# Paged attention in a four-layer kernel: cached values fetched by SyncE, one transfer a page, instead of by GpSimd gathers of rows

## The reference

```python
B, S, HID = (4, 128, 512); D, HQ, HK = (128, 32, 8); PAGES, PSIZE, NPP = (64, 32, 16)
q, k, v = projections of x by Wq, Wk, Wv; q and k: RMS norm, then rotary embedding
kc = k_cache[block_table].reshape(bsz, L, HK, D)
vc = v_cache[block_table].reshape(bsz, L, HK, D)
k_all = jnp.concatenate([kc, k], axis=1)
v_all = jnp.concatenate([vc, v], axis=1)
scores = jnp.einsum('bqhd,bkhd->bhqk', q, k_all) * SCALE
scores = jnp.where(valid[:, None, None, :], scores, -1e+30)
probs = jax.nn.softmax(scores, axis=-1)
o = jnp.einsum('bhqk,bkhd->bqhd', probs, v_all)
return jnp.einsum('bse,de->bsd', o.reshape(bsz, seqlen, HQ * D), Wo)
```

## Time and profile before

| | |
|---|---|
| median of three runs | 3655.53 us |
| the profiled execution | 3660.96 us |
| its span, first to last instruction | 3659.2 us |
| mean granted TensorE clock | 0.964 |
| TensorE busy, of the span | 3193.8 us, 87% |
| VectorE, ScalarE, GpSimd busy | 1825.0, 1293.9, 1583.7 us |
| SyncE's own queue (q1), packets and bytes | 363540, 197.79 MB |
| GpSimd's queue (q0), packets and bytes | 50768, 175.71 MB |

### The profile page before, as it was taken

One profiled execution on the slowest core, in us unless ns is written; L12 is line 12 of the kernel. 1 busy time (PEld: TensorE's weight loads), 2 busy tenths in 40 slices (PEclk: granted clock), 3 DMA queues, 4 the chain that ended last, 5 costly groups with the idle time before them and its releaser, 6 DMA issues. The chain is left out here.

```text
span 3659.2 us, 66283 instructions
## 1 busy us (share of the span) xinstructions
PE 3193.8 (87%) x15248; PEld 2058.2 (56%) x15248; DVE 1825.0 (50%) x5079; ACT 1293.9 (35%) x3541; POOL 1583.7 (43%) x1336
## 2 busy tenths in 40 slices
PE   3599999999999999989999999999999976888887
PEld 2366666666666656556566666666566553444444
DVE  4254554555555555554545455445445534555555
ACT  1234443444344443433343344334433321222222
POOL 7444455555555555554555545545554410000000
PEclk8799999999999999999999999999999997999898
DMA  5533333333333333543333333333333333111110
GB/s 192 201 96 109 105 104 106 107 109 105 104 107 116 109 110 112 175 149 105 105 104 104 104 104 106 113 109 113 111 111 106 98 125 97 29 34 49 31 29 12
DMA packets 415398, 376.22 MB, mean 103 GB/s; under 512 B 83364, under 2 KB 346292, under 8 KB 414277
## 3 DMA queue, kind: packets, MB, share of 16 engines
q1 hardware_dynamic: 363540, 197.79, 18.6%
q0 software_dynamic: 50768, 175.71, 15.5%
q10 hardware_dynamic: 864, 0.63, 0.1%
HBM read 340.37 MB, written 25.17 MB: 100 GB/s over the span
## 5 line engine op out<-in xcount | busy, mean ns | idle before, releaser
L355 PEld LDWEIGHTS ps_oT<-pT,v_sb 128*128 128x128 f32 x4096 | 525.7, 195 | 427.3 <-ACT pT L425 248.4
L417 ACT ACTIVATE p_sb<-s_sb,nmax 128x544 f32<-128x544 f32 x512 | 383.2, 748 | 1017.4 <-DVE nmax L516 907.9
L355 PE MATMUL ps_oT<-pT,v_sb 128*128 128x128 f32 x4096 | 579.1, 285 | 176.7 <-ACT pT L425 145.5
L288 PE MATMUL ps_t<-wqkv,xT 128*128 128x512 f32 x1536 | 694.5, 595 | 7.6 <-DMA xT<-x1T_scratch 7.6
L182 POOL DMA_INDIRECT v_sb<-in_v_rows_w,v_row x512 | 507.2, 991 | 289.0 <-issue 127.4
L516 DVE CUSTOM_DVE_ANT_0 s_sb<-ps_s,mask,nmax_new 128x416 f32<-128x416 f32 x512 | 333.4, 651 | 353.6 <-PE ps_s L329 281.4
L312 PE MATMUL ps_t<-wo,oT 128*128 128x512 f32 x1024 | 449.9, 592 | 0.4 <-ACT oT L433 0.4
L329 PE MATMUL ps_s<-k_sb,qT 128*128 128x416 f32 x1024 | 445.9, 523 | 0.0
L288 PEld LDWEIGHTS ps_t<-wqkv,xT 128*128 128x128 f32 x1536 | 278.9, 191 | 288.4 <-issue 280.6
L197 POOL TENSOR_SCALAR ss<-ss 128x12 f32<-128x12 f32 x64 | 13.2, 206 | 965.3 <-DVE ss L494 962.8
L532 DVE TENSOR_SCALAR p_sb<-p_sb,rinv 128x544 f32<-128x544 f32 x512 | 370.0, 723 | 18.1
(11 more groups left out here) (214 smaller groups left out, 4282.5 us busy)
## 6 DMA issues: line engine op xcount, KB each, us to landing
k_sb<-in_kT SPq DMA_DIRECT2D x2048, 64.0 KB
xT<-x1T_scratch POOLq DMA_DIRECT2D x32, 256.0 KB
tab<-rope_scratch POOLq DMA_DIRECT2D x32, 256.0 KB
v_sb<-in_v_rows_w,v_row POOLq DMA_INDIRECT x512
wo<-in_wo_w POOLq DMA_DIRECT2D x2, 4096.0 KB, 15.6
v_new<-v_raw SPq DMA_DIRECT2D x128, 64.0 KB
y_scratch<-y_sb SPq DMA_DIRECT2D x32, 256.0 KB
wqkv<-in_wqkv_w SPq DMA_DIRECT2D x6, 1024.0 KB, 9.0
```

What stands on the lines that cost most here:

```text
L288: m = e.matmul(ps_t[bank_of(t)][:, :], xT[:, k, :], wqkv[:, k, 512 * t:512 * t + 512], start=k == 0, stop=k == KC - 1)
L355: e.matmul(ps_oT[:, :], v_sb[:, b % 2, c, h * D:(h + 1) * D], pT[:, u % 2, c, :], start=c == 0, stop=False)
L417: e.activation(p_sb[:, u % 2, :], s_sb[:, u % 2, :], ACT.Exp, bias=nmax[:, u % 2:u % 2 + 1], scale=-1.0, accum_out=rsum[:, u % 2:u % 2 + 1 ...
```

## The change

The cached values are no longer gathered by GpSimd. SyncE issues them, right after the keys of the same block, from the page numbers that it already holds in registers: 16 transfers of one page, 32 tokens x 512 values, into 32 of the 128 partitions of `v_sb`. Before them it waits until the block before last is weighed. The cache of values is laid out by page and half of the heads, as that of the keys was. What served the row numbers goes: `btx`, `voff`, `v_rows`, `v_row`, two GpSimd instructions and two loads in `embed`, and a copy a round. TensorE's wait for a block's values counts 16 transfers instead of 4.

```diff
@@ attention, SyncE @@
                     wait(e, scored, UNITS * r + HKH * (b - 1))
                     for j, page in enumerate(pages):
                         e.dma_start(k_sb[:, b % 2, j, :, :], A["kT"][bass.ds(page * HALVES + half, 1), :, :, :].rearrange("a d h s -> (a d) h s")).then_inc(dma_k[b % 2], 16)
+
+                    wait(e, weighed, UNITS * r + HKH * (b - 1))
+                    for j, page in enumerate(pages):
+                        at = slice(PSIZE * (j % LC), PSIZE * (j % LC) + PSIZE)
+                        e.dma_start(v_sb[at, b % 2, j // LC, :], A["v_pages"][bass.ds(page * HALVES + half, 1), :, :].rearrange("a s n -> (a s) n")).then_inc(dma_v[b % 2], 16)
@@ attention, GpSimd @@
-            def load_rows(r):
...
-            def load_v(r, b):
-
-                wait(e, weighed, UNITS * r + HKH * (b - 1))
-                e.sem_inc(passed, 1)
-                for c in range(LC):
-                    e.indirect_dma_start(out=v_sb[:, b % 2, c, :], out_offset=None, in_=A["v_rows_w"],
-                                         in_offset=bass.IndirectOffsetOnAxis(ap=v_row[:, b, c:c + 1], axis=0)).then_inc(dma_v[b % 2], 16)
-
...
                 if last(r):
-                    load_v(r, 2)
-                    load_v(r, 3)
                     return
-                rotate(r + 1, 0, lambda: load_v(r, 2))
-                load_v(r, 3)
+                rotate(r + 1, 0)
                 rotate(r + 1, 1)
-                load_rows(r + 1)
-                load_v(r + 1, 0)
 
                 e.wait_ge(raw_copied, NT * (r + 2))
                 if xg is not None:
                     load_x(xg)
                 if weights:
                     load_w(1)
-                load_v(r + 1, 1)
@@ attention, TensorE @@
                 if h == 0:
-                    e.wait_ge(dma_v[b % 2], 16 * LC * (2 * r + b // 2 + 1))
+                    e.wait_ge(dma_v[b % 2], 16 * NPP * (2 * r + b // 2 + 1))
@@ embed, GpSimd @@
-            for h in range(HALVES):
-                step(e.tensor_scalar(v_rows[:, h * B * LC:(h + 1) * B * LC], btx[:, h, :], float(PSIZE * HALVES), voff[:, h:h + 1], ALU.mult, ALU.add))
@@ laid_out @@
-    a["v_rows_w"] = i["L1_cond_v_cache"].reshape(PAGES * PSIZE * HALVES, HKH * D)
+    a["v_pages"] = i["L1_cond_v_cache"].reshape(PAGES, PSIZE, HALVES, HKH * D).transpose(0, 2, 1, 3).reshape(PAGES * HALVES, PSIZE, HKH * D)
```

More of the change, by code:

```diff
@@ L37, with attention @@
 NEG = -1e30
-def attention(nc, sb, pb, sem, wqkv, wo, dma_wqkv, dma_wo, x1T_d, tab_d, y_d, A, ident, iota, seqf, v_rows, load_beside):
+def attention(nc, sb, pb, sem, wqkv, wo, dma_wqkv, dma_wo, x1T_d, tab_d, y_d, A, ident, iota, seqf, load_beside):
     k_sb = sb("k_sb", [P, 2, NPP + 1, HKH, PSIZE], F32)
@@ L44, in attention @@
     bt = sb("bt", [1, B * NPP], I32)
-    v_row = sb("v_row", [P, GB, LC], U32)
     xT = sb("xT", [P, KC, P], F32)
@@ L82, in attention @@
     dma_vn, v_cleared = sem("dma_vn"), sem("v_cleared")
-    new_scored, new_copied, new_ready, placed, rows_ready = (sem(n) for n in ("new_scored", "new_copied", "new_ready", "placed", "rows_ready"))
+    new_scored, new_copied, new_ready, placed = (sem(n) for n in ("new_scored", "new_copied", "new_ready", "placed"))
     dma_k = [sem(f"dma_k{i}") for i in range(2)]
@@ L188, in _, with rotate @@
             parts = [[(0, 12, 0)], [(12, HQH - 12, 0), (HQH, HKH, 2)]]
-            def rotate(r, i, gathers=None):
+            def rotate(r, i):
                 h0, h1 = ((0, 12), (12, HT))[i]
@@ L213, in rotate @@
                     if half:
-                        if gathers is not None:
-                            gathers()
                         e.wait_ge(rope_step, done)
@@ L249, in _ @@
             e.wait_ge(half_made, 1)
-            load_rows(0)
-            load_v(0, 0)
-            load_v(0, 1)
             e.dma_start(wo[:, :, :], A["wo_w"][0]).then_inc(dma_wo[0], 16)
@@ L570, with embed @@
 XB = 4
-def embed(nc, sb, pb, sem, wqkv, dma_wqkv, A, x1_d, x1T_d, tab_d, ident, seqf, v_rows):
+def embed(nc, sb, pb, sem, wqkv, dma_wqkv, A, x1_d, x1T_d, tab_d, ident, seqf):
     qw = sb("qw", [P, KC, HID], I32)
@@ L600, in embed @@
     tabs = sb("tabs", [P, GROUPS, 4, D], F32)
-    btx = sb("btx", [P, HALVES, B * LC], I32)
-    voff = sb("voff", [P, HALVES], F32)
     seqi = sb("seqi", [P, HALVES * B], I32)
@@ L699, in step @@
                 e.wait_ge(chain_p, done[0])
-            e.wait_ge(dma_t, 16 * 6)
+            e.wait_ge(dma_t, 16 * 4)
             e.wait_ge(dma_c, 32)
@@ L772, in _ @@
         def _(e):
-            for to, of in ((posi, "seq_tok"), (invf, "inv_freq"), (w4, "rope_w"), (btx, "bt_rows"), (voff, "row_off"), (seqi, "seq_all")):
+            for to, of in ((posi, "seq_tok"), (invf, "inv_freq"), (w4, "rope_w"), (seqi, "seq_all")):
                 e.dma_start(to[:], A[of]).then_inc(dma_t, 16)
@@ L1368, in program @@
         seqf = sb("seqf", [P, HALVES * B], F32)
-        v_rows = sb("v_rows", [P, HALVES * B * LC], U32)
         dma_const = sem("dma_const")
@@ L1390, in program @@
                 sb, pb = tools(ctx)
-                embed(nc, sb, pb, sem, wqkv, dma_wqkv[0], A, x1_d, x1T_d, tab_d, ident, seqf, v_rows)
+                embed(nc, sb, pb, sem, wqkv, dma_wqkv[0], A, x1_d, x1T_d, tab_d, ident, seqf)
             with ExitStack() as ctx:
                 sb, pb = tools(ctx)
-                attention(nc, sb, pb, sem, wqkv, wo, dma_wqkv, dma_wo, x1T_d, tab_d, y_d, A, ident, iota, seqf, v_rows, load_beside)
+                attention(nc, sb, pb, sem, wqkv, wo, dma_wqkv, dma_wo, x1T_d, tab_d, y_d, A, ident, iota, seqf, load_beside)
             with ExitStack() as ctx:
@@ L1421, in laid_out @@
     a["inv_freq"] = rows((np.float32(1.0) / np.float32(10000.0) ** (np.arange(0, D, 2, dtype=np.float32) / np.float32(D))).astype(np.float32))
-    a["row_off"] = np.stack([(tok % PSIZE) * HALVES + h for h in range(HALVES)], 1).astype(np.float32)
     a["c_identb"] = np.eye(P, dtype=np.float32).astype(mybir.dt.np(BF))
@@ L1443, in laid_out @@
     a["block_table"] = bt.reshape(1, B * NPP)
-    a["bt_rows"] = np.repeat(np.repeat(bt.reshape(B * LC, P // PSIZE), PSIZE, axis=1).T[:, None, :], HALVES, axis=1)
     qn, kn = HQH * D, HKH * D
```

## The result

| | before | with the change |
|---|---|---|
| median | 3654.26 us (4 runs) | 4421.94 us (4 runs, 4417.09 to 4423.66) |
| span of the profiled execution | 3659.2 us | 4421.3 us |
| attention stage ends at | 3015.0 us | 3778.1 us |
| mean granted TensorE clock | 0.964 | 0.888 |

The change makes the kernel slower by a factor of 1.21 (95% interval 1.2079 to 1.2121), 768 us. The direction was forecast, and so was what sets the new time: SyncE's queue.

What follows compares the result with a forecast made beforehand. SyncE and TensorE were taken to share the bound. 1352 us of added transfers, less 37 of waits filled and 6 at the stage's end, gave +1309 us: 4965 us for the median, range 4480 to 5150 us.

Steps and rivals of the forecast that it cites:

- The bound: In the attention stage SyncE, with 1.1 us of waiting a round, is as full as TensorE; the two share the bound.
- The price of a page of values: On SyncE in the attention stage: 2048 added transfers at 0.66 us each, 1352 us.
- rival A: A page of values is issued on SyncE at the price of a page of keys, 0.44 us: 4514 us; chance 0.19.
- What else SyncE does: SyncE's existing 87.96 us a round stays, and the values' transfers bring it to 130.2 us.
- the sum: Values' transfers less waits filled and the stage's earlier end: 1352 - 37 - 6 = +1309 us.
- a possible surcharge on the values: 8% of unnamed stalls, seen in SyncE's bursts of keys, put on the values: 0.71 us a transfer, 1454 us.
- The waits filled: The values' transfers fill SyncE's present waits on TensorE in the attention stage: -36.6 us.
- The end of the stage: From SyncE's last transfer to the attention stage's end: 28.7 us instead of 34.7, 6 us less.
- The new wait: SyncE's wait, ahead of the values, for the block before last to be weighed: met on arrival, nothing taken.
- rival B: SyncE also stands at the new wait because TensorE, partly at a lower clock, weighs late: 5093 us; chance 0.11.
- TensorE's clock: In the attention stage the granted clock falls in pauses of some 42 us a round; nothing in the sum.
- Nothing for GpSimd's relief: 512 gathers of 957 ns leave GpSimd in the attention stage; taken to gain nothing.

Runs made afterwards that it cites:

- the doses above: The changed kernel with 16 page-number loads a block but no bounds check: 3899.24 us; with one load of 16 registers a block instead: 3591.18 us.

## Why the prediction was right or wrong

- **The bound** was read rightly, and the change is slower by the mechanism that was forecast. SyncE, which has no row in the table of busy times, shared the bound with TensorE, and the doses above show its instructions setting the time.
- **The price of a page of values** is the larger of the two terms that failed: "I take 0.66: two of three neighbours have the few long rows of the values". It is 0.464 us from one to the next in a burst, 960 us in all bursts in place of 1352: 392 too many. By itself this would have given 4573 us, within the range. The few rows were the wrong likeness. `c_B2g` paid for the 512-piece transfer ahead of it and `v_new` for its source in SBUF. The third neighbour, the page of keys, for which 0.44 was worked out, was the right one: an address in a register, HBM to SBUF, and in bursts. That was rival A, given 0.19; a page of values takes 37 ns more than a page of keys in the kernel, 370 against 333.
- **What else SyncE does** is the second term that failed: the sum adds the values' price to SyncE's work of before and takes that work as fixed. It shrank by 162 us, since the gathers had delayed it. The prediction saw the bursts of 9.93 and 8.92 us against 8.20 and said that the trace does not name the cause. It counted them as a possible surcharge on the values, and at the lower ends of its ranges let them shrink by 80 us, or by 30 us in rival A, never in the sum. The long steps lay beside gathers, which a look at both timelines together would have shown, and the change takes the gathers away. This is why even rival A's 4514 us was too high, and why the time fell below the range.
- **The waits filled** were forecast at 37 us and were 35. **The end of the stage** is 34.1 us behind SyncE's last transfer (3744.0 to 3778.1), where 28.7 were forecast and 34.7 stood before: no gain. The forecast let the last values land in 2.2 us. The last of them, issued at 3743.6, landed at 3753.2, more than 9 us later, among some 5 MB of weights that GpSimd was fetching for the tail, and TensorE stood for them:

```profile
3753.24 2.08 PE L331 MATMUL ps_oT<-pT,v_sb 128*128 128x128 f32 x8 [6.49 <-DMA v_sb<-in_v_pages]
```

- **The sum** as measured: 960 - 162 - 35 - 1 = 762 us, the difference of the spans.
- **The new wait** is met on arrival, 1.8 us in all: rival B did not come about.
- **TensorE's clock** fell as forecast, to 0.91 over a round, and stayed behind SyncE: TensorE stood for keys all the same, 26 us a round rather than 42, as the round is 18 us shorter than forecast.
- **Nothing for GpSimd's relief**: right for TensorE's path; on chips with the long steps it was wrong by way of SyncE.
- The Trainium skill's "usually small relative to the DMA itself" (DMA: Bandwidth & Descriptors, "Issuing engines are not separate DMA queues") misleads here. One issue is a quarter of the way to the landing, 0.464 against 1.8 us. But the landings of a burst overlap and the issues do not, and 2048 of them in a full queue cost 960 us.

## What to carry to other kernels

Sum up what a queue's instructions take, register loads and checks included, before you give it more: SyncE's 88 us a round stood in no table, and some 40 of them were register loads that one instruction of 1 us a block replaces. Price a transfer by one between the same two memories, with a like number of pieces and in the same surroundings, and look at what stands ahead of the one that you take the price from. And when a change takes work off one engine, look whether that work slows another one down now, even one that never waits for it.

## What was not expected of the hardware

- Issuing one transfer from SyncE, address in a register, HBM to SBUF: 369 or 370 ns in a burst with 16 or 32 rows, 381 with 128, and 316 behind a register load (16 and 32 rows). At a fixed address the instruction takes 421 to 432 ns, but from one to the next it is the same 0.46 to 0.47 us, since no move stands between. From SBUF to SBUF it takes 590 ns, with 512 pieces 550 to 580, and a short transfer right behind such a one 560.
- One register load of 16 values takes 977 ns. Sixteen single ones take 0.63 us each, from one to the next, with their arithmetic and check, and 0.38 without the check.
- On one chip, or two, SyncE's instructions are held for about 0.7 us at a time beside GpSimd's gathers (281 and 311 such steps in the kernel before); on two others they are not (2 and none).
